# Edge MLP of a graph network: who makes the turned one-hots, and in how many instructions

## The reference, cut to what matters

```
row, col = src, dst
e = silu(concat(h[row], h[col]) @ We1 + be1)      # 100000 x 64
e = silu(e @ We2 + be2)                           # 100000 x 64
agg = segment_sum(e, row, num_segments=6250)
out = silu(concat(h, agg) @ Wn1 + bn1) @ Wn2 + bn2
x = layernorm(x + h + out)
```

## Time and profile before

| | us |
|---|---|
| median of 3 runs | 5642.28 |
| lowest and highest | 5641.04, 5644.34 |
| the profiled execution's own time | 5646.53 |
| its span, first to last instruction | 5644.7 |
| edge MLP, from its first gather to the next stage's first transposes | 2442.65 to 3486.6 |

### The profile page before, as it was taken

The page is one execution under the profiler, slowest core; times in us unless marked ns, Lnnn a source line. Parts: engine busy times, 40 slices in busy tenths (PEclk is TensorE's granted clock), DMA queues, the critical chain, the costliest instruction groups (busy, mean ns, idle before and its releaser), DMA issues. The chain is left out here.

```text
span 5644.7 us, 81221 instructions
## 1 busy us (share of the span) xinstructions
PE 3161.6 (56%) x17051; PEld 2754.3 (49%) x17052; DVE 3215.2 (57%) x10738; ACT 1491.8 (26%) x5626; POOL 3915.3 (69%) x4054
## 2 busy tenths in 40 slices
PE   4444444356666666678888988444444443444443
PEld 3333333345555555667777777333333443333332
DVE  5877777576777777743433344544444444444445
ACT  2333434345555555532212122200000000000001
POOL 3777777736777777457777774477777757777774
PEclk7555555567788877765555556755566555565556
DMA  5222222214444444222222220111121122211122
GB/s 123 53 53 53 53 52 57 47 51 130 131 131 131 132 132 130 75 55 52 52 52 53 55 52 22 55 53 53 52 52 53 52 62 53 53 53 52 52 53 58
DMA packets 222221, 385.58 MB, mean 68 GB/s; under 512 B 85452, under 2 KB 121882, under 8 KB 221998
## 3 DMA queue, kind: packets, MB, share of 16 engines
q0 software_dynamic: 142944, 296.35, 20.6%
q1 hardware_dynamic: 79054, 86.72, 5.1%
HBM read 356.23 MB, written 26.56 MB: 68 GB/s over the span
## 5 line engine op out<-in xcount | busy, mean ns | idle before, releaser
L2247 POOL DMA_INDIRECT arena<-table_gcn,idx_now x1568 | 1487.8, 949 | 642.5 <-issue 422.4
L2297 PE MATMUL pair<-arena,hotf 128*128 x3328 | 751.9, 418 | 1143.1 <-POOLq L1820 1120.2
L2297 PEld LDWEIGHTS pair<-arena,hotf 128*128 128x128 f32 x3328 | 702.0, 320 | 1185.6 <-issue 1185.6
L2314 DVE TENSOR_SCALAR hotf<-iota,rel_now,ew_now 128x128 f32<-128x128 f32 x1664 | 443.6, 365 | 1038.0 <-PE pair L2300 1038.0
L664 POOL DMA_INDIRECT arena<-table_attention,idx_now x832 | 814.7, 979 | 273.8 <-issue 206.6
L664 POOL DMA_INDIRECT arena<-table_key_value,idx_now x832 | 789.1, 948 | 276.2 <-issue 221.5
L1855 POOL DMA_INDIRECT arena<-table_edge_mlp,idx_now x784 | 780.6, 996 | 261.2 <-issue 219.4
L1071 PE MATMUL pair<-wide,hotf 128*128 128x130 f32 x1664 | 427.7, 436 | 646.7 <-ACT wide L1035 646.7
L1071 PEld LDWEIGHTS pair<-wide,hotf 128*128 128x128 f32 x1664 | 366.2, 324 | 711.4 <-ACT wide L1035 711.4
L2257 ACT COPY idx_now<-src_t 128x8 int32 (+1 forms) x204 | 39.3, 197 | 1773.4 <-PE pair L2300 1761.5
L1994 DVE TENSOR_TENSOR hot<-pair,arena 128x64 f32<-128x64 f32 x832 | 134.4, 225 | 549.5 <-POOLq L1820 530.4
(11 more groups left out here) (371 smaller groups left out, 5647.1 us busy)
## 6 DMA issues: line engine op xcount, KB each, us to landing
key<-rel_dram SPq DMA_DIRECT2D x104, 256.0 KB, 3.5
arena<-rel_dram SPq DMA_DIRECT2D x52, 512.0 KB
arena<-table_gcn,idx_now POOLq DMA_INDIRECT x1568, 2.5
arena<-table_attention,idx_now POOLq DMA_INDIRECT x832, 2.6
arena<-table_key_value,idx_now POOLq DMA_INDIRECT x832, 2.9
arena<-table_edge_mlp,idx_now POOLq DMA_INDIRECT x784, 2.5
table_attention<-arena SPq DMA_DIRECT2D x13, 512.0 KB, 2.9
table_gcn<-acc SPq DMA_DIRECT2D x26, 256.0 KB, 2.3
```

The source lines that it names most:

```text
L2247: q_.indirect_dma_start(conv_ring[:, slot * D:(slot + 1) * D], None, table, bass.IndirectOffsetOnAxis(ap=idx_now[:, slot:slot + 1].bitcast ...
L2297: t_.matmul(window[:, bass.ds(offset * D, D)], hot8[:, g % 2, u, :], conv_ring[:, bass.ds(slot * D, D)], start=False, stop=False)
L2314: last = v.tensor_scalar(out=hot8[:, g % 2, u, :], in0=iota[:, :], scalar1=rel_now[:, at], scalar2=ew_now[:, at], op0=ALU.is_equal, op1=AL ...
```

## The change

The turned one-hots of the edge MLP are no longer made by DVE in one comparison, but by ACT in two instructions: Abs of `part - rel_rows`, written over `rel_rows` in place, and the maximum of 0 and 1 minus that, written to `hotT8` as bf16. Between the two ACT waits for its own first one (`l2_away`). ACT does this after its second SiLU and ahead of its copies for GpSimd; the first three groups stand ahead of `silu1(0)`. The waits for SP's broadcast and for PE's use of the buffer (`l2_look`) move to ACT with it.

```diff
+                def hot_look(k, g):
+                    away = rel_rows[:, g % 4 // 2, g % 2 * CG * P:(g % 2 + 1) * CG * P]
+                    act.wait_ge(l2_rel_in[g % 4 // 2], 16 * (k // 4 + 1) if isinstance(k, int) else 4 * k - 4 * (g % 4) + 16)
+                    s_.activation(away, away, ACT.Abs, scale=-1.0, bias=part[:, 0:1]).then_inc(l2_away, 1)
+                    at_least(act, l2_look, k, -1)
+                    act.wait_ge(l2_away, k + 1)
+                    s_.activation(hotT8[:, g % 2, :], away, ACT.Relu, scale=-1.0, bias=ones[:, 0:1]).then_inc(l2_hotT, 1)
...
                     s_.activation(s2[:, g % 2, :], EB, ACT.Silu).then_inc(l2_s2, 1)
+                    if not isinstance(k, int) or k + 3 < CSTEP_GROUPS:
+                        hot_look(k + 3, g + 3)
                     if not isinstance(k, int) or k + LAG + 1 < CTILE_GROUPS:
                         place_tiles(k + LAG + 1, (g + LAG + 1) % CRING)
...
                 last.then_inc(l2_placed, 1)
+                for k in range(3):
+                    hot_look(k, k)
                 silu1(0, 0)
...
-                def hot_look(i, g, k):
-                    dve.wait_ge(l2_rel_in[g % 4 // 2], 16 * (k // 4 + 1) if isinstance(k, int) else 4 * k - 4 * (g % 4) + 16)
-                    at_least(dve, l2_look, k, -1)
-                    v.tensor_scalar(out=hotT8[:, g % 2, :], in0=rel_rows[:, g % 4 // 2, g % 2 * CG * P:(g % 2 + 1) * CG * P], scalar1=part[:, 0:1], scalar2=None,
-                                    op0=ALU.is_equal).then_inc(l2_hotT, 1)
...
                 def step(i, g, k):
-                    if not isinstance(k, int) or k + 3 < CSTEP_GROUPS:
-                        hot_look(i, g + 3, k + 3)
                     if not isinstance(k, int) or k + 2 < CSTEP_GROUPS:
                         before_silu(i + (g + 2) // CRING, (g + 2) % CRING, k + 2)
...
-                for k in range(3):
-                    hot_look(0, k, k)
                 for k in range(2):
                     before_silu(0, k, k)
```

More of the change, by code:

```diff
@@ L1834, in at_least @@
                 eng.wait_ge(signal, k + more)
-        l2_landed, l2_clear = sem("l2_landed"), sem("l2_clear")
+        l2_landed, l2_clear, l2_away = sem("l2_landed"), sem("l2_clear"), sem("l2_away")
         (l2_placed, l2_hotT, l2_look, l2_pre, l2_s1, l2_s1T, l2_s1T_kept, l2_e, l2_s2, l2_same, l2_sum, l2_acc) = (
```

## The result

| | us |
|---|---|
| kernel before, median of 12 runs (5639.6 to 5647.1) | 5641.8 |
| changed kernel, median of 12 runs (5651.7 to 5661.6) | 5654.6 |
| ratio, 95% interval | 1.0023 (1.0015 to 1.0032) |
| forecast, and its range | 5619, 5607 to 5638 |
| profiled executions, before and changed | 5646.5, 5661.6 |

The changed kernel is 13 us slower, where I had forecast 23 us faster. It lies outside the range. The profiled execution of the changed kernel is the slowest of its 12 runs.

The account below looks back on a forecast made before the run. GpSimd's gathers were taken to pace the edge MLP. The profiled 5646.53 us minus 23.2 for stretched gathers, other terms 0, gave 5623.3; minus 4.25, as the median lies below the profiled run, 5619.1; range 5607 to 5638.

Parts of the forecast that it names:

- Moved: Edge MLP: ACT's later one-hot is ready 0.26 us (0.1 to 0.4) before PE takes up own_half; nothing booked.
- Removed from DVE: Edge MLP: without DVE's 104 comparisons, 84 stretched gathers return to 0.94 us, a gain of 23.2 us.
- What stays: Edge MLP: hot_sum (line 2000) keeps its place and its 16.8 us of stretched gathers; change taken as 0.
- rival 1: Edge MLP: line 2000 takes over stretching gathers, giving back up to 22 of 23.2 us, so 5641; chance 0.08.
- Added on ACT: Edge MLP: Abs and Relu at 1.12 us each plus a 0.2 wait, 2.44 us a step, covered.
- Start of the stage and SP: Edge MLP: three first pairs on ACT, 7.3 us, and SP's later reload of rel_rows are covered, costing nothing.
- Rival 2: Edge MLP: PE becomes the bound if its step needs 1 us more; 5620 to 5628; chance 0.08.
- Rival 3: Edge MLP: ACT loads tables twice a step between Abs and SiLU, 43 us longer, 5685; chance 0.06.
- Rival 4: Edge MLP: DVE's clearing of line 2012, not the comparison, stretches the gathers, so nothing goes, 5642; chance 0.06.
- my tests: Edge MLP signs: line 1855's mean falls from 996 to about 965 ns, PE's turn waits from 133 to about 110 us.
- My test for a missed margin: Edge MLP sign: a PE wait of own_half for ACT's Relu would say that the 0.26 us margin was missed.

Follow-up runs that it names:

- e9: Kernel before, with DVE's comparison made to wait for one spare Abs on ACT; 5645.1 us, ratio 0.9998.
- e2: Kernel before, with DVE's comparison made to wait for a spare Abs and Relu on ACT; 5710.6 us, ratio 1.0111.
- e4: Changed kernel, with own_half's node tiles at fixed addresses and no register instructions among its products (output not the reference's); 5614.5 us, ratio 0.9943.
- e1: Changed kernel, with ACT making the one-hot ahead of its second SiLU instead of behind it; 5633.2 us, ratio 0.9969 to the kernel before.
- e3: Kernel before plus a spare Abs and Relu on ACT for which DVE does not wait; 5648.4 us, ratio 1.0000.
- e7: Kernel before with hot_sum's constant read from PSUM; ratio 1.0074, on a chip where the kernel before itself took 6851 to 6865 us.

## Why the prediction was wrong

**The step that failed** is *Moved*, where I wrote "The margin is 0.26 us" and "I book nothing". The margin was measured to the moment when PE's array takes up `own_half`. The array did take it up in time; the sequencer did not. The sequencer reaches the wait for the one-hot 2.3 us before the array gets to `own_half`, and the semaphore has to be up 1.84 us before (e9, e2, the changed kernel), or the 24 register instructions are no longer covered by `summed`. The one-hot came 0.43 ahead, so `own_half` took 1.4 us more in the step shown and 1.2 on average, 297.7 - 170.6 = 127 us of PE. The stage's balance, busy time by stretch of the changed kernel (PE, PEld, DVE, ACT, POOL; clock, DMA share, GB/s), against the earlier trace rows:

```profile
2443.00:3503.00 1060.00, 1035.32 (x5618) 870.68 (x5619) 372.50 (x1142) 426.42 (x715) 769.90 (x784) 0.50 0.21 51
```

PE is busy for 1035 us instead of 902, 134 more, and idle for 24 of 1059 instead of 142 of 1044, 119 less. The 15 us between the two are the loss: PE's slack took up all that it could. The granted clock, 0.50 against 0.51, is the lower level in both. The sign was there in the code: `own_half` is 24 short products with addresses from registers, and I had priced only what the array does with them. It was in the trace too, in the 3.26 us of the kernel before's second `own_half` (at e4).

The Trainium skill describes the parts: in "Advanced Engine Details and Errata", section Sequencer and Instruction Queues, a sequencer reads instructions and pushes them into a queue from which the engine takes them, and PE's runs at its own clock. The traces agree with such a queue: the first register instruction of `own_half` starts 2.3 us ahead of its first weight load in the kernel before. They put 3.1 to 3.2 us on the 24 register instructions.

**Removed from DVE** was right as a mechanism. No gather is held under a comparison any more, 84 before. In e1, where PE has its slack back, the gain is 16 us where I had 23. **What stays** was sized wrong: I took 0 for `hot_sum`'s share, and its held gathers went from 16.2 to 29.8 us in the changed kernel, and to 30.7 in e1. In the changed kernel the additions ahead of it waited for `own_half` 67 times, so that it no longer starts at a landed count but often wherever PE lets DVE go. In e1 it starts at the landed count again (547.1 us of waits for it), and why more gathers are held there is open. One of the longest now:

```profile
3438.86 1.22 DVE L2006 TENSOR_TENSOR hotf<-iota,rel_now 128x1024 f32<-128x1024 f32 x1
...
3438.96 1.93 POOL L1855 DMA_INDIRECT arena<-table_edge_mlp,idx_now  x1 [0.30 <-issue]
```

3438.96 + 1.93 is 0.81 after 3438.86 + 1.22, the same distance as before. That was rival 1 in mechanism, and its bound of 22 us more held: 13.6 and 14.5 us more here. By its trace this cost the changed kernel nothing, as PE was the bound, but no run shows that. **Added on ACT**: 1.14 and 1.15 us against my 1.12, and 0.09 us of wait between them against 0.2; e3 shows the load free. **Start of the stage and SP**: no new delay; the first `turn` starts 13.8 us behind the first gather in both. **Rival 2**, PE as the bound, is what happened, with a chance of 0.08 and a price that was too low, since I let PE's delay begin only where the margin ends. **Rival 3**: one table load, as forecast. **Rival 4** is out: the clearings of line 2018 are still there and hold nothing. Of my tests, the mean of line 1855 was to fall to about 965 ns and fell to 982, through `hot_sum`; PE's waits at `turn` were to fall to about 110 us and fell to 8.1. My test for a missed margin, a wait of `own_half` for the Relu, could not have shown this: the loss stands under no wait of PE.

## What to carry to other kernels

When an input of a PE section is moved later, measure its slack to where the sequencer reaches the wait, not to where the array starts; a section with register addresses needs its semaphores up ahead of that, here 1.84 us, and the trace shows the shortage as products that last the same but follow more slowly, under no wait at all. Where a queue of gathers on GpSimd is the pace, look at the gathers' own lengths: mean against median finds what holds them, and giving an offending DVE instruction on two SBUF operands one of them from PSUM cost one copy here. Of two changes that move work off the busy path, try the place in the order first; here one line further up was worth 29 us.

## What the runs showed of the hardware that I had not expected

The bf16 comparison of 428 ns held 84 gathers when it stood directly behind another DVE instruction, but none in e2 and 2 in e9, where it came after a wait. There it was the comparison that took longer, 495 and 500 ns on average instead of 428:

```profile
L1998 DVE TENSOR_SCALAR hotT<-arena,part 128x1024 bf16<-128x1024 bf16 x104 | 51.5, 495 | 533.2 <-ACT arena L1890 528.3 <-DMA arena<-rel_dram 3.0 <-PE pair L1938 1.9
```

I read this as the two taking turns, where who comes first depends on what stands before; no run tests it. `hot_sum` looks alike: where it starts 0 to 0.33 us after a gather it holds nothing (64 times in the kernel before), and the gathers that it holds started up to 1.07 us after it.

In the executions of 6850 us and more there are stretches in which PE's instructions come one every 1.2 us or more, each under "issue", and others at the usual pace. In e7 190 such pauses of over 0.9 us fall into the stage, 71 of them in `own_half`, many of the others ahead of products with fixed addresses; the kernel before has 2. First PE alone in such a stretch of e7, then its register instructions in the same step:

```profile
3500.45 0.22 PE L1926 MATMUL pair<-arena,hotT 128*128 x1 [1.20 <-issue]
3502.55 0.21 PE L1926 MATMUL pair<-arena,hotT 128*128 x1 [1.88 <-issue]
...
L1926 PEldq FUSED_REGOPS  x16: 8/46/712, 3494.0 to 3503.2; - x16
```

A register instruction takes up to 712 ns there instead of 46: in e7 84 of 3190 take over 600 ns, in the kernel before none of 3467. The kernels are the same as in the executions of 5645 us, so something outside them slowed the issuing of instructions. Which kernel is best depends on it, and its cause was not found.
